# Feed-forward joins, the statistics of steps 41 and 42, and the back transposes of steps 34 to 42 in other slots

## The chip, the cores and the metric

One core of a Trainium2 chip runs the whole program. The metric is the device time of one launch in microseconds. The kernel before has a median of 708.54 us over three runs (708.42 to 709.91).

## The reference

The reference is a decoder block over four batches of 512 tokens with 512 features, in float32. There are 16 heads of 32 features, and every attention is causal.

```
x = x + self_attention(layernorm(x))          # q, k, v, o projections with biases
x = x + cross_attention(layernorm(x), ctx, ctx)   # no projections, keys and values are ctx
x = x + ffn(layernorm(x))
ffn(x) = relu(x @ W_up.T) @ W_down.T + sum(softmax(top2(x @ W_gate.T))) * (x @ W_expert)
```

## The kernel before

All engines follow one hand-made timetable of steps and slots. A step is one pair of heads (64 of them: 32 groups of four heads, two steps each), and has 8 slots, one for each head of the pair and block of 128 queries. The number of a slot is z = 8 * step + slot; below, "slot 41.5" is slot 5 of step 41. A slot is a place in each engine's program, not a time. Each engine runs its own program in order, and waits on semaphores for the others.

In slot i of step s:
- TensorE computes the score tile i of pair s + 1 (L500) into one of three banks, then runs what `RUNNING` gives it (a quarter of a projection or feed-forward job, "fill"; one quarter is three matmuls of 512 columns, or four transposes), and then turns a tile of probabilities of pair s (L514, four to one transposes) into a bank `t` or a free bank `m`.
- VectorE masks and reduces the score tile (L716), copies the turned tiles of slots 2, 3, 6 and 7 (L726), and empties the banks of jobs (`empty`).
- ScalarE takes the exponential (L944), copies the turned tiles of slots 0, 1, 4 and 5 (L953), and copies the high parts of the operands.
- GpSimd scales the probabilities of self-attention, makes the keys of cross-attention (`keys`, L1090 and L1092), and adds the result to the residual (`added`, L1100).
- SyncE issues the DMAs. `load_stack(s + 2)` lays out the operands of the scores two steps ahead.

At slot 0 of each even step TensorE first runs the **values burst** (`values`, L547: 16 small matmuls, 32 records), which closes the group of the two steps before. For a cross group ScalarE then copies it to `cn` in slot 2 (`context_hi`, L970), TensorE transposes it back into the same bank (`back`, L657, end of slot 4), VectorE scales it (`back_scaled`, L846, slot 5), and GpSimd adds it in the next step. In odd steps TensorE turns the queries of a coming group (`queries`, slot 1, L568), ScalarE and VectorE copy their high and low parts (`query_hi` in slot 3, L1007; `query_lo` in slot 5, L838). The values burst of the next even step waits for that `query_lo`, since both use the bank `pv`.

Cross-attention of batch f is done after step 8 (f + 5). Then its feed-forward part is fed in, one batch per eight steps: `f_stats_slots` (L750, L752) and `f_norm_slots` (L779) on VectorE, with `f_scale` on GpSimd (L1074, L1076) between them, then four turns of the normalised rows (`FL`, L568, at `turns_at`), whose high part ScalarE copies (L979) and whose low part VectorE subtracts (L802), then the gate (`FG`, L619), the up projection (`FU`), the expert (`FE`) and the down projection (`FD`), each in four jobs of four slots. The feed-forward matmuls are L553 to L555. VectorE adds the results of FE and FD to the residual (L828, L834). The jobs share two banks `m0` and `m1`: `plan()` gives each job the bank that is free first, and makes it wait until the job before it in that bank has been emptied. Score turns get a bank `m` where none of the jobs is near, else `t0` and `t1` in turn. `plan()` gives every job the same bank before and after the change; 147 of the 512 turns get another one, all from slot 42.5 on.

The normalisation ahead of cross-attention (`stats_slots`, `norm_slots`, L743 and L771) of batch j - 4 runs in the same way, with `ln_scale` (L1070) on GpSimd. The last group of batch 0 is 19 (steps 38 and 39, its back transposes in step 40). `f_stats_of(0, 0)` waits until GpSimd has added it.

## Time and profile before

| | us |
|---|---|
| median of three runs | 708.54 |
| lowest, highest | 708.42, 709.91 |
| profiled execution, time | 706.88 |
| profiled execution, span of the core | 705.0 |
| TensorE busy | 672.6 |
| ScalarE busy | 501.6 |
| VectorE busy | 494.4 |
| GpSimd busy | 257.1 |

All times in the rows below are counted from the start of the span of the profiled execution. The names PE, DVE, ACT and POOL are TensorE, VectorE, ScalarE and GpSimd. A row of a stretch (rows 2 and 4) has its borders and length, then busy time and instructions of PE, PEld (the weight loads), DVE, ACT and POOL, then PEclk, the busy share of the DMA engines and GB/s. A row of a timeline has start, length, engine, line, instruction and how many are merged. A value in square brackets is the idle time of the engine just before the instruction, with what ended it. PEclk is the granted TensorE clock as a share of 2.4 GHz.

### The profile page before, as it was taken

To read this page: it belongs to the slowest core of one execution; us is meant where nothing else is said; L and a number is where in the kernel's file an instruction comes from. 1 tells how busy PE (TensorE), PEld (TensorE's weight loads), DVE (VectorE), ACT (ScalarE), POOL (GpSimd) and SP (SyncE) were. 2 spreads that over 40 slices of the span, in tenths; PEclk is the share of its full clock that TensorE was granted. 3 is DMA by queue.
4 is the path that set the end of the run, shared out by engine and by line. 5 is a ranking of instruction groups with operands and counts; after the bars stand their busy time and mean duration, and the time that the engine had idled before them with its cause. 6 is when DMAs were issued, how large, how long until landed. Compare 5 with 4: busy or idle time off the path is not lost.

```text
span 705.0 us, 13884 instructions
## 1 busy us (share of the span) xinstructions
PE 672.6 (95%) x4488; PEld 520.1 (74%) x4488; DVE 494.4 (70%) x1730; ACT 501.6 (71%) x1450; POOL 257.1 (36%) x391
## 2 busy tenths in 40 slices
PE   6998999999999999999978988999999999999998
PEld 5776777777877777677756765777767887777786
DVE  6668766766766676767878779978867777764632
ACT  5778877777876778787898878877768876763110
POOL 4745645333555345751654432553202102000100
PEclk9999999999999999999999999999999999999999
DMA  9753533336433464354955776464435344320101
GB/s 315 193 151 75 141 70 91 77 93 184 117 71 91 127 196 98 88 123 124 268 140 144 195 215 144 120 166 104 113 98 156 100 105 106 69 96 1 59 1 60
DMA packets 52326, 86.12 MB, mean 122 GB/s; under 512 B 8608, under 2 KB 16800, under 8 KB 52256
## 3 DMA queue, kind: packets, MB, share of 16 engines
q1 hardware_dynamic: 52256, 85.25, 46.0%
q8 instruction: 36, 0.59, 0.3%
q14 instruction: 34, 0.28, 0.1%
HBM read 27.55 MB, written 7.34 MB: 49 GB/s over the span
## 4 chain that ended last, share of the span: by engine, by line
PE 80%; ACT 7%; DVE 6%; issue 2%; DMA 2%; POOL 2%; SPq 1%; ACTq 0%; POOLq 0%; DVEq 0%
PE t L514 15%; PE m L553 14%; PE m L554 14%; PE m L555 14%; PE pv L547 10%; PE s L500 8%; ACT probs L944 3%; DVE probs L716 2%; PE m L514 2%; ACT prob L953 2%; PE m L619 1%; DMA stack<-stage 1%; POOL probs L1057 1%; PE m L568 1%; DVE prob L726 1%
## 5 line engine op out<-in xcount | busy, mean ns | idle before, releaser
L716 DVE CUSTOM_DVE_ANT_0 probs<-s,mask 128x128 f32<-128x128 f32 (+3 forms) x512 | 246.5, 483 | 124.2 <-PE s L500 122.0
L944 ACT ACTIVATE probs<-probs,negmax 128x128 f32<-128x128 f32 (+3 forms) x512 | 284.7, 559 | 44.3 <-DVE negmax L716 43.6
L514 PE MATMUL t<-ident,probs 128*128 128x128 f32 x1116 | 198.0, 276 | 10.6 <-ACT prob L953 7.1
L500 PE MATMUL s<-stack 96*128 96x128 f32 (+3 forms) x512 | 196.5, 392 | 2.9 <-DMA stack<-stage 1.7
L1057 POOL TENSOR_SCALAR probs<-probs,rsum 128x128 f32<-128x128 f32 (+3 forms) x256 | 133.4, 539 | 176.4 <-DVE rsum L730 176.0
L953 ACT ACTIVATE prob<-t 128x384 f32<-128x384 f32 (+1 forms) x225 | 121.5, 541 | 87.1 <-PE t L514 85.5
L514 PEld LDWEIGHTS t<-ident,probs 128*128 128x128 f32 x1116 | 140.5, 141 | 57.4 <-ACT prob L953 11.0
L500 PEld LDWEIGHTS s<-stack 96*128 96x128 f32 x512 | 97.4, 190 | 14.1 <-DMA stack<-stage 2.4
L944 ACT ACTIVATION_READ_ACCUMULATOR probs<-probs,negmax 128x1 f32 x512 | 99.1, 194 | 0.0
L726 DVE COPY prob<-t 128x256 f32<-128x256 f32 (+1 forms) x215 | 76.3, 355 | 29.8 <-PE t L514 29.1
L553 PE MATMUL m<-xT_hi,w_lo 128*128 128x512 f32 x192 | 78.4, 409 | 1.2 <-DVE xT_lo L784 1.2
L554 PE MATMUL m<-xT_lo,w_hi 128*128 128x512 f32 x192 | 75.8, 395 | 0.0
L555 PE MATMUL m<-xT_hi,w_hi 128*128 128x512 f32 x192 | 75.6, 394 | 0.0
L553 PE MATMUL m<-w_hi,xT_lo 128*128 128x512 f32 x128 | 52.8, 413 | 0.0
L554 PE MATMUL m<-w_lo,xT_hi 128*128 128x512 f32 x128 | 50.5, 394 | 0.0
L555 PE MATMUL m<-w_hi,xT_hi 128*128 128x512 f32 x128 | 50.2, 393 | 0.0
L555 PEld LDWEIGHTS m<-xT_hi,w_hi 128*128 128x128 f32 x192 | 36.1, 188 | 8.6
L716 DVE DVE_READ_ACCUMULATOR2_ANT negmax<- 128x1 f32 x512 | 42.4, 83 | 0.0
L547 PE MATMUL pv<-prob,cv 128*32 128x128 f32 (+3 forms) x512 | 39.4, 450 | 1.6 <-ACT prob L953 1.4
L553 PEld LDWEIGHTS m<-xT_hi,w_lo 128*128 128x128 f32 x192 | 36.8, 191 | 2.7 <-DVE xT_lo L784 1.4
L554 PEld LDWEIGHTS m<-xT_lo,w_hi 128*128 128x128 f32 x192 | 36.5, 190 | 2.9
L547 PE MATMUL pv<-prob,V 128*32 128x128 f32 (+3 forms) x512 | 37.8, 435 | 0.0
(144 smaller groups left out, 956.6 us busy)
## 6 DMA issues: line engine op xcount, KB each, us to landing
stack<-stage SPq DMA_DIRECT2D x384, 128.0 KB, 2.3
xt<-in_x SPq DMA_DIRECT2D x16, 256.0 KB, 4.2
xres<-in_x SPq DMA_DIRECT2D x4, 1024.0 KB, 6.0
kraw<-in_ctxT SPq DMA_DIRECT2D x16, 256.0 KB, 3.0
cv<-in_ctx SPq DMA_DIRECT2D x16, 256.0 KB, 3.3
x<-xres SPq DMA_DIRECT2D x3, 1024.0 KB, 5.8
res<-x SPq DMA_DIRECT2D x8, 256.0 KB, 6.3
out<-res SPq DMA_DIRECT2D x2, 1024.0 KB, 4.7
```

The costliest lines, as they stand in the source:

```text
L500: nc.tensor.matmul(score_tile(P, i), stack[0:RS, P % 2, h, 0, chunk(qb)], stack[0:RS, P % 2, h, 1, 0:N], start=True, stop=True).then_inc(s ...
L514: mm = nc.tensor.transpose(dst[:, chunk(qb - kb)], probs[:, (2 * P + h) % 3, OFF[qb] + PART * kb:OFF[qb] + PART * kb + PART], ident[:, :])
L547: mm = nc.tensor.matmul(pv_bank[HD * j:HD * j + HD, PART * kb:T], v[:, HD * j:HD * j + HD], prob[kb][:, j, :], start=(kb == 0), stop=(kb = ...
L553: nc.tensor.matmul(dst, lhs[1], rhs[0], start=(c == 0), stop=False)
L554: nc.tensor.matmul(dst, lhs[0], rhs[1], start=False, stop=False)
L555: return nc.tensor.matmul(dst, lhs[0], rhs[0], start=False, stop=(c == KC - 1))
L568: mm = nc.tensor.transpose(dst[:, chunk(t)], src[:, t, chunk(c)], ident[:, :])
L716: nc.vector.tensor_tensor_reduce(probs[:, (2 * P + h) % 3, OFF[qb]:OFF[qb + 1]], score_tile(P, i), mask[:, T - N:T], -SCALE, BIG, ALU.add, ...
L726: nc.vector.tensor_copy(prob[kb][:, 2 * (P % 2) + h, :], turned_tile(P, i)).then_inc(t_dve, 1)
L944: nc.scalar.activation(tile, tile, ACT.Exp, bias=negmax[:, P % 2, h, qb:qb + 1], scale=-1.0, accum_out=total).then_inc(p_exp, 1)
L953: nc.scalar.activation(prob[kb][:, 2 * (P % 2) + h, :], turned_tile(P, i), ACT.Copy).then_inc(t_act, 1)
L1057: nc.gpsimd.tensor_scalar(tile, tile, rsum[:, P % 2, h, qb:qb + 1], 0.0, ALU.mult, ALU.add).then_inc(p_done, 1)
```

## The change

Five things move, all in the timetable; the arithmetic is the same.

- `back_slot`: the back transposes of the groups that end in steps 34 to 42 run in slot 5 instead of slot 4, and their scaling on VectorE in slot 6 instead of 5 (groups 16, 18, 19 and 20).
- The statistics of batch 0's feed-forward move from slots 41.1, 41.2, 41.4, 41.5 to 41.4, 41.6, 42.0, 42.0, its normalisation from 42.0, 42.0, 42.1, 42.1 to 42.4, 42.5, 42.6, 42.6. `f_scale(0)` on GpSimd moves from the end of step 41 into step 42, ahead of the wait for the normalisation and of `keys(23)`.
- The turns FL of batches 0, 1 and 2 start one slot later (from 43.1, 51.1, 59.1), the gate two slots later (44.4, 52.4, 60.4).
- The up projection follows: for batches 0 and 1 its four jobs start at 45.0, 45.5, 46.1, 46.6 instead of 44.6, 45.3, 46.0, 46.5, and the expert where it did (47.2); the last down job starts one slot later (51.6 instead of 51.5). For batch 2 all jobs from the gate on are two slots later.
- The statistics of batch 1's second norm move from 43.1 to 43.2 (the first one), its normalisation from 44.1, 44.4, 44.4, 44.5 to 44.3, 44.4, 44.5, 44.6.

```diff
--- before.py
+++ after.py
@@ -92,6 +92,11 @@
     return 2 * RANK[P // 2] + P % 2
 
 
+def back_slot(s):
+
+    return 3 if s >= NP else 5 if NPS + 2 <= s < PAIRS * (B + 1) + 3 else 4
+
+
 def feed_start(f):
 
     return FEED[f]
@@ -99,13 +104,13 @@
 
 def turns_at(f):
 
-    u = feed_start(f)
+    u = feed_start(f) + 1
     return [u + 3 * m for m in range(KC)]
 
 
 def gate_at(f):
 
-    return feed_start(f) + (8 if f == B - 1 else 10)
+    return feed_start(f) + (8 if f == B - 1 else 12)
 
 
 def route_at(f):
@@ -115,7 +120,7 @@
 
 def up_at(f, m):
 
-    return gate_at(f) + 4 + (4 if f >= B - 2 else 5) * m
+    return gate_at(f) + 4 + 4 * m + (0 if f >= B - 2 else (m + 1) // 2)
 
 
 def expert_at(f, m):
@@ -127,7 +132,7 @@
 
     if f >= B - 2:
         return expert_at(f, KC) + 4 * m
-    return expert_at(f, KC) + 5 * m if m < 2 else feed_start(f + 1) + 5 * (m - 2)
+    return expert_at(f, KC) + 5 * m if m < 2 else feed_start(f + 1) + 6 * (m - 2)
 
 
 def stats_slots(j):
@@ -137,7 +142,7 @@
         z -= 2 * PAIRS if j == B else 0
         return [z - 8, z - 7, z, z + 1]
     if j == B + 2:
-        return [z + 25, z + 28, z + 29, z + 31]
+        return [z + 26, z + 28, z + 29, z + 31]
     return [z, z, z + 16, z + 16] if j == B + 1 else [z, z, z + 1, z + 1]
 
 
@@ -149,20 +154,20 @@
     if j == B:
         return [z + 2, z + 3, z + 5, z + 6]
     if j == B + 2:
-        return [z + 33, z + 36, z + 36, z + 37]
+        return [z + 35, z + 36, z + 37, z + 38]
     return [z + 32, z + 32, z + 33, z + 33]
 
 
 def f_stats_slots(f):
 
     z = PAIRS * (PAIRS * (f + B + 1) + 1)
-    return [z + 1, z + 2, z + 4, z + 5]
+    return [z + 4, z + 6, z + 8, z + 8] if f == 0 else [z + 1, z + 2, z + 4, z + 5]
 
 
 def f_norm_slots(f):
 
     z = PAIRS * (PAIRS * (f + B + 1) + 2)
-    return [z, z, z + 1, z + 1]
+    return [z + 4, z + 5, z + 6, z + 6] if f == 0 else [z, z, z + 1, z + 1]
 
 
 END = (feed_start(B - 1) + UNITS) // PAIRS + 1
@@ -702,7 +707,7 @@
                             turn_gate(f)
                     if s % 2 == 1 and other((s + 3) // 2) and i == 1:
                         queries((s + 3) // 2)
-                    if s % 2 == 0 and other(s // 2 - 1) and i == (4 if s < NP else 3):
+                    if s % 2 == 0 and other(s // 2 - 1) and i == back_slot(s):
                         back(s // 2 - 1)
 
 
@@ -913,7 +918,7 @@
                         query_lo((s + 3) // 2)
                     if s % 2 == 0 and other(s // 2 - 1) and i == 1:
                         c_recip(s // 2 - 1)
-                    if s % 2 == 0 and other(s // 2 - 1) and i == (5 if s < NP else 4):
+                    if s % 2 == 0 and other(s // 2 - 1) and i == back_slot(s) + 1:
                         back_scaled(s // 2 - 1)
                     for j in range(1, 2 * B):
                         for t in range(NT):
@@ -1141,6 +1146,8 @@
                 if own(s // 2):
                     for qb in range(NT):
                         scaled(s, 1, qb)
+                if s == f_stats_slots(0)[-1] // PAIRS:
+                    f_scale(0)
                 for j in range(B + 1, 2 * B):
                     if s == norm_slots(j)[-1] // PAIRS:
                         pool.wait_ge(ln_done, NT * (j + 1))
@@ -1157,7 +1164,7 @@
                 for j in range(1, 2 * B):
                     if s == stats_slots(j)[-1] // PAIRS:
                         ln_scale(j)
-                for f in range(B):
+                for f in range(1, B):
                     if s == f_stats_slots(f)[-1] // PAIRS:
                         f_scale(f)
                 if 3 <= s < 3 + NT:
```

## Rows read from the trace of the kernel before

**Rows 1.** The page's section 1: busy time and share of the span.

```profile
PE 672.6 (95%) x4488; PEld 520.1 (74%) x4488; DVE 494.4 (70%) x1730; ACT 501.6 (71%) x1450; POOL 257.1 (36%) x391
```

**Rows 2.** Busy time by stretch, steps 41 to 44, one step a row.

```profile
417.30:424.41 7.11, 5.34 (x35) 3.85 (x33) 7.01 (x28) 7.11 (x24) 1.28 (x1) 1.00 1.05 288
424.41:433.88 9.47, 8.29 (x65) 5.16 (x65) 8.06 (x29) 6.27 (x21) 3.17 (x4) 0.82 0.66 158
433.88:442.47 8.59, 6.72 (x47) 5.02 (x46) 8.39 (x29) 8.59 (x28) 1.28 (x1) 1.00 0.34 86
442.47:453.57 11.10, 10.66 (x87) 8.00 (x88) 10.84 (x36) 9.31 (x29) 5.65 (x8) 1.00 0.54 131
```

**Rows 3.** TensorE's timeline, steps 40 to 44: start, length, instruction, idle before.

```profile
415.68 0.33 PE L657 MATMUL pv<-ident,cn 128*128 128x128 f32 x1 [0.90 <-ACT cn L970]
...
422.77 0.44 PE L500 MATMUL s<-stack 96*128 96x384 f32 x1 [0.86 <-DVE negmax L716]
...
424.41 0.30 PE L500 MATMUL s<-stack 96*128 96x128 f32 x1 [0.62 <-DMA stack<-stage]
...
432.20 0.33 PE L657 MATMUL pv<-ident,cn 128*128 128x128 f32 x1 [0.92 <-ACT cn L970]
...
448.29 0.50 PE L619 MATMUL m<-xT_hi,g_both 128*128 128x512 f32 x1 [0.43 <-ACT xT_hi L979]
```

**Rows 4.** Two stretches with granted clock; the values bursts of steps 42 and 44.

```profile
421.50:424.90 3.40, 1.73 (x9) 1.02 (x9) 3.33 (x13) 3.40 (x12) 0.00 (x0) 1.00 1.01 216
424.90:428.30 3.40, 3.33 (x20) 1.13 (x24) 3.37 (x12) 1.50 (x6) 1.29 (x2) 0.50 0.63 146
...
424.96 4.01 PE L547 MATMUL pv<-prob,cv 128*32 128x512 f32 x32 [0.26 <-DVE stage L838]
...
442.70 2.36 PE L547 MATMUL pv<-prob,cv 128*32 128x512 f32 x32
```

**Rows 5.** VectorE's timeline from the first statistics of batch 0 to step 42.

```profile
419.62 0.69 DVE L750 BATCH_NORM_STATS2 f_stats<-xt 128x6 f32<-128x512 f32 x1
...
420.44 0.53 DVE L716 CUSTOM_DVE_ANT_0 probs<-s,mask 128x384 f32<-128x384 f32 x1
...
424.18 0.68 DVE L838 TENSOR_TENSOR stage<-pv,stage 128x512 fp32r<-128x512 f32 x1
...
426.99 0.29 DVE L726 COPY prob<-t 128x128 f32<-128x128 f32 x1
...
427.40 1.00 DVE L779 TENSOR_SCALAR f_xln<-xt,f_mv,f_rstd 128x512 f32<-128x512 f32 x2
429.73 0.42 DVE L716 CUSTOM_DVE_ANT_0 probs<-s,mask 128x256 f32<-128x256 f32 x1 [1.33 <-PE s L500]
```

**Rows 6.** ScalarE's timeline: the query copy of step 41.

```profile
422.67 0.60 ACT L1007 ACTIVATE stage<-pv 128x512 fp32r<-128x512 f32 x1
```

**Rows 7.** VectorE's timeline, norms in step 44; GpSimd splits weights from 446.71 to 450.66.

```profile
446.78 0.82 DVE L771 TENSOR_SCALAR V<-res,mv,rstd 128x512 f32<-128x512 f32 x1 [0.19 <-POOL rstd L1070]
...
449.94 1.46 DVE L771 TENSOR_SCALAR V<-res,mv,rstd 128x512 f32<-128x512 f32 x2
```

**Rows 8.** TensorE's timeline in steps 51, 52 and 59.

```profile
512.76 0.44 PE L568 MATMUL m<-ident,f_xln 128*128 128x128 f32 x2 [0.76 <-DVE xt L834]
...
516.60 0.40 PE L553 MATMUL m<-w_hi,w_lo 128*128 128x512 f32 x1
...
517.07 0.40 PE L555 MATMUL m<-w_hi 128*128 128x512 f32 x1
517.65 0.66 PE L568 MATMUL m<-ident,f_xln 128*128 128x128 f32 x4 [0.18 <-DVE xT_lo L802]
...
519.60 0.51 PE L553 MATMUL m<-w_hi,w_lo 128*128 128x512 f32 x1 [0.55 <-DVE xt L834]
...
528.43 0.74 PE L619 MATMUL m<-xT_hi,g_both 128*128 128x512 f32 x2 [0.19 <-DVE xt L834]
...
594.30 0.55 PE L568 MATMUL m<-ident,f_xln 128*128 128x128 f32 x3 [0.76 <-DVE res L834]
```

## The prediction, made before the change was run

> **What bounds the kernel now.** I read the page's first section, then the engines in stretches one step long, then each engine's own timeline where TensorE stood still. The page shows TensorE busy for 95% of the span, with VectorE and ScalarE at 70% and 71% [rows 1]. So over the whole span an edit pays only where it takes idle time off TensorE, or lets the engine that starves it finish earlier. I took the first score matmul of each step as the step's start (the start times are the borders in [rows 2]). By that the steps that the change touches are of two kinds.
>
> Steps 41 to 44 are not bound by TensorE. In step 41 it works 5.34 us of 7.11, in 42 8.29 of 9.47, in 43 6.72 of 8.59. VectorE works 7.01 of 7.11, 8.06 of 9.47, 8.39 of 8.59 and, in step 44, 10.84 of 11.10 [rows 2]. VectorE stands still for only 0.10 + 1.41 + 0.20 + 0.26 = 1.97 us in four steps. ScalarE has no idle time at all in steps 41 and 43. The TensorE stalls here (0.90, 0.86, 0.62, 0.92, 0.43 us [rows 3]) are therefore mostly a symptom: they can only be gained so far as VectorE and ScalarE also get ahead. Steps 51, 52, 59 and 60 are different: there TensorE has no other idle time than a few stalls behind the chain of feed-forward banks [rows 8], and the others have room. In steps 45 to 50 and 53 to 58 the timeline shows no stall of TensorE at all, so nothing can be gained there.
>
> **The clock.** From 424.9 to 428.3 us the granted clock is 0.50, the lower level of 1.2 GHz, after a stretch in which TensorE worked 1.73 of 3.40 us [rows 4]. The values burst that opens step 42 fell into it and took 4.01 us; the same 32 matmuls took 2.36 us at the full clock, so 1.65 us went to it.
>
> **Part 1: back transposes one slot later (steps 34, 38, 40, 42).** A back transpose waits for ScalarE's copy cn. The wait is 0.90 us in step 40 and 0.92 us in step 42 [rows 3]; the back transposes of 34 and 38 show no idle time at that line, so I cost them at nothing (34 and 35 wait for GpSimd, 38 is full). One slot later, the score tile and turn of slot 5 stand ahead of it and cover the 0.9 us. But ScalarE runs without a gap after each values burst, and TensorE catches up with it in the next step. I count 0 for the removed waits themselves, with 1.8 us as the other end. The scaling goes behind one more score tile and copy on VectorE (about 0.8 us later); who waits for it is the query transpose of slot 1 in the next step and GpSimd's addition, and neither stands behind it in the trace of before, so I cost that at nothing; if the room is gone, it is those 0.8 us.
>
> **Part 2: statistics of batch 0 from slots 41.1, 41.2, 41.4, 41.5 to 41.4, 41.6, 42.0, 42.0.** One costs VectorE 0.82 us (419.62 to 420.44 [rows 5]). Ahead of query_lo in slot 41.5 stood three, now one, so VectorE could start it 1.64 us sooner than 424.18, at 422.54. But query_lo waits for ScalarE's query copy, 422.67 + 0.60 = 423.27 [rows 6], and ScalarE is gapless. So query_lo moves by 0.91 us, not 1.64. Behind it the count of statistics ahead of the copy of slot 41.7 (426.99) is unchanged, so that ends at 427.28 - 0.91 = 426.37. Then one score tile (0.2) and the two statistics of 42.0 (1.64) fill the time in which TensorE runs the values burst: VectorE is ready at 428.2, where before it stood idle for 1.33 us and resumed at 429.73 [rows 5]. TensorE's burst ends near 427.0 if the clock stays up, near 427.8 if it falls again; either way VectorE is last. **Gain at the start of slot 42.1: 1.5 us.**
>
> **Part 3: normalisation of batch 0 from 42.0, 42.0, 42.1, 42.1 to 42.4 to 42.6.** Two of the four stood in the burst's shadow (1.00 us for two at 427.40 [rows 5]). Now all four stand behind it, on an engine that has 0.2 us to spare until step 44: a loss of 1.0 us. What remains when the values burst of step 44 ends is 1.5 - 1.0 = **0.5 us**. f_scale is two small operations on a GpSimd that works 3.17 of 9.47 us in step 42 [rows 2], and four score tiles of VectorE (0.3 to 0.6 us each) stand between the statistics and slot 42.4, so I count no wait. GpSimd's wait for f_xln now holds back keys(23) by half a step; the stack load that needs them is issued in step 44, so that is at nothing too.
>
> **Part 4: joins of batch 0 one to two slots later.** The gate's wait for xT_hi (0.43 us, at 448.29 [rows 3]) has one more slot of distance and goes. Two job slots of the up projection leave step 44 for steps 45 and 47. A job slot is three matmuls at 0.235 us (516.60 to 517.07 for two [rows 8]), 0.7 us. TensorE's step 44 gets 1.4 us lighter than VectorE's 10.84 us, so VectorE bounds it, and the 0.7 us that land past step 45 are paid there: up to 0.7 us back. Against it VectorE's own waits in step 44 (0.26 us) go, and its norms shift away from GpSimd's weight split: beside it they took 0.82 and 1.46 us for three, where one alone takes 0.5 [rows 5, 7], so about 0.7 us of VectorE time may come back. The Trainium skill has this as a lock (SBUF — State Buffer, on the port pair that DVE and GpSimd share: a VectorE operation in a two-port mode and one of GpSimd block each other for its whole length). The trace fits it: norms over-long only where GpSimd works. Part 4 sums to 0.43 + 0.26 + 0.7 - 0.7 = 0.7 us at best and -0.3 at worst; I take **0.4 us**. Steps 41 to 47 together: 0.5 + 0.4 = **0.9 us**.
>
> **Part 5: joins of batches 1 and 2 (steps 51, 52 and 59, 60).** The first turn of the next batch waits 0.76 us for a bank that VectorE empties at slot 51.0; in slot 51.1 a turn, a score tile and a down slot (some 1.6 us) stand ahead: gone. The last down job waits 0.55 us for its bank, one slot more: gone. The gate waits 0.19 us, one slot more: gone. That is 1.50 us. Against it: the second turn waited 0.18 us for xT_lo although the last down slot (0.7 us) stood between them in slot 51.3 [rows 8]. In slot 51.4 it stands alone behind a score tile. That cover is lost, and the copy ahead is 0.15 us shorter: the stall grows to 0.18 + 0.7 - 0.15 = 0.7, so 0.5 to 0.6 us is given back. Net 0.95 us per pair of steps, bounds 0.8 and 1.5. Steps 59 and 60 run the same program for the next batch and show the same stall of 0.76 us at its place [rows 8]: **1.9 us** for both. Batch 2's two job slots that move behind step 63 are work of the same length in another place.
>
> **The sum.** 0.9 + 1.9 = 2.8 us. The profiled execution has a span of 705.0 and a time of 706.88 us, 1.66 us under the median of the three runs, 708.54; some run-to-run difference of this size (one fallen clock stretch is worth as much) is there. I apply the 2.8 us to the median: 708.54 - 2.8 = **705.7 us**, and a new span near 702.2 beside a profile like this one.
>
> **The rivals.** *All that TensorE waits for is gained.* Then 0.90 + 0.86 + 0.62 + 0.92 + 0.43 = 3.7 us, the clock's 1.65 and twice 1.50, or 8.4 us: 700.1. For it: the stalls stand on the very engine that is busy for 95%. Against: VectorE's 1.97 us of idle time in steps 41 to 44 is all that can be taken there unless its work shrinks. Chance 0.10; half-way to it lies 702.8.
> *The new stalls eat the gain.* The second turn's wait takes over what the first gives (0.3 us left each time), and in 41 to 47 the norms' 1.0 us and the up slots' 0.7 us cancel the 1.5: 708.0, within 0.2%. That the slots were already covered, so that nothing moves, ends here too. Chance 0.25.
> *Slower: VectorE in steps 42 to 45.* If ScalarE's query copy comes no sooner and VectorE's two statistics outlast the burst, nothing is gained at 42.1, and the 1.0 us of norms and the 0.7 us of up slots are paid in full; with batches 1 and 2 at nothing the time is 708.54 + 1.7 = 710.2. It decides once VectorE resumes after the burst of step 42 later than 1.0 us after TensorE offers it the score tile. The clock adds to it: TensorE would stand still for 3 us in step 43 instead of 1.87, and a stretch at 0.5 there costs up to 1.65 us. Chance 0.15.
>
> **How the numbers follow.** The forecast (704 to 707.1) has 0.50, the full gain 0.10, no difference 0.25, slower 0.15. The lower end takes in half of the full gain (702.8), the upper one the no-difference case and part of the slower one (709.2). What a measurement can tell from no change is 0.2%, 1.4 us: faster 0.60, same 0.25, slower 0.15.
>
> **What would show it.** In the trace after: no wait of the back transposes for cn in steps 40 and 42; query_lo of step 41 right behind ScalarE's copy; two statistics in the shadow of the values burst and no VectorE idle time there; VectorE busy for all of step 43, and the burst of step 44 ending about 0.5 us sooner. In steps 51 and 59 the first turn and the last down job without a wait, and the second turn with one of 0.6 to 0.8 us. If TensorE's idle time in step 43 grows while the step ends later, the slower case holds; if the second turn waits no longer than before, the gain is nearer to 4 us.

## The result: 0.25% slower

The changed kernel has a median of 709.69 us over 21 runs (707.59 to 711.93), the kernel before beside it 708.38 us, also over 21 (705.51 to 711.59). The ratio is 1.0025, with a 95% interval of 1.0013 to 1.0036 (the two medians by themselves give 1.0018). The prediction was 705.7 us, with a range of 702.8 to 709.2. The profiled execution has a time of 708.46 us and a span of 706.6. Two executions of the kernel before beside the experiments took 838 and 1097 us at a mean granted clock of 0.75 and 0.56, and no figure here counts them.

The page's section 1 for the changed kernel answers to [rows 1]:

```profile
PE 672.4 (95%) x4488; PEld 520.3 (74%) x4488; DVE 492.1 (70%) x1730; ACT 501.6 (71%) x1450; POOL 257.2 (36%) x391
```

All engines run the same instructions, and none is busy for longer by more than 0.2 us; what grew is time in which TensorE waits. The busy times by step, 41 to 47, with columns as in [rows 2]:

```profile
417.43:425.26 7.83, 5.25 (x35) 3.79 (x33) 6.97 (x27) 7.83 (x25) 1.28 (x1) 1.00 1.05 310
425.26:432.25 6.99, 6.67 (x64) 4.69 (x65) 6.89 (x28) 5.37 (x19) 1.29 (x2) 1.00 1.03 225
432.25:441.36 9.11, 6.70 (x47) 5.13 (x45) 8.34 (x30) 9.11 (x29) 3.14 (x3) 1.00 0.35 89
441.36:451.86 10.50, 9.29 (x77) 6.41 (x78) 10.20 (x32) 7.91 (x26) 5.18 (x6) 1.00 0.60 138
451.86:462.03 10.17, 9.45 (x58) 7.72 (x58) 8.61 (x34) 8.69 (x27) 7.61 (x9) 1.00 0.34 82
462.03:473.26 11.23, 11.23 (x87) 8.32 (x86) 6.20 (x27) 7.56 (x22) 2.96 (x3) 1.00 0.77 209
473.26:482.45 9.19, 9.01 (x55) 7.37 (x54) 7.16 (x27) 7.43 (x23) 8.43 (x9) 1.00 0.28 71
```

Steps 45 and 47 of the kernel before, for comparison:

```profile
453.57:461.69 8.12, 8.12 (x54) 6.92 (x52) 7.71 (x30) 6.97 (x22) 7.88 (x8) 1.00 0.54 148
472.92:481.05 8.13, 8.13 (x53) 6.94 (x51) 5.75 (x23) 6.65 (x21) 7.27 (x8) 1.00 0.32 81
```

Step 42 is 2.5 us shorter and step 44 0.6 us, but step 45 is 2.05 us longer, 47 1.06, 41 0.72 and 43 0.52. The table sets the lengths beside those of all experiments. A length is from the first score matmul of a step to that of the next, read off each trace. The last three columns are sums; step 40 takes 7.43 us with the back transposes in their old slot and 6.98 in the new one. Kernels marked * had TensorE's granted clock at 0.50 for 3.4 or 6.8 us in steps 41 to 43. So columns 41 to 43 are to be compared among those without a mark.

```
us                      step 41    42    43    44    45    46    47 | 40-43  44-47  51-56
before *                   7.11  9.47  8.59 11.10  8.11 11.23  8.13 | 32.60  38.57  62.91
loads_later                7.11  8.24  8.59 11.10  8.11 11.23  8.13 | 31.37  38.57  62.90
after                      7.83  6.99  9.11 10.50 10.17 11.23  9.19 | 30.91  41.09  63.36
joins_only                 7.34  7.94  8.66  9.61 10.18 11.25  9.19 | 31.37  40.23  63.38
joins_before               7.14  7.79  9.84 11.19  8.11 11.23  8.14 | 31.75  38.67  62.91
back_only                  8.40  7.51  8.60 11.16  8.12 11.23  8.15 | 31.49  38.66  62.91
stats_only *               8.08  9.20  9.92 11.18  8.11 11.23  8.14 | 34.63  38.66  62.88
loads_and_back             7.39  8.24  8.59 11.10  8.11 11.23  8.15 | 31.20  38.59  62.91
loads_later_back_stats *   5.90  9.41  9.83 11.96  8.11 11.23  8.15 | 32.12  39.45  62.89
after_loads_later *        5.90  8.69 10.21 10.56 10.19 11.25  9.20 | 31.78  41.20  63.36
no_m_turns                 7.58  7.77  8.60 11.10  8.11 11.23  8.14 | 31.37  38.58  62.93
gate_one *                 8.99  8.63  9.12 11.98 10.46 11.19  8.12 | 33.72  41.75  63.37
one_gate_moved             5.90  8.68  9.29 11.81  9.92 11.22  8.14 | 30.85  41.09  62.93
up_before *               10.51  9.74  9.11 11.79  9.92 11.22  8.14 | 36.34  41.07  64.40
norm6_before *             8.05  8.69  9.12 10.00 10.16 11.25  9.20 | 32.84  40.61  63.34
norm6_only                 7.11  8.24  8.60 11.73  8.11 11.23  8.14 | 31.37  39.21  62.88
norm7_earlier *            8.47  9.73  9.12 10.47 10.18 11.25  9.19 | 34.30  41.09  62.98
f_norm_earlier *           8.74  9.64  8.93 10.48 10.19 11.25  9.20 | 34.29  41.12  63.35
```

The row loads_later is the kernel before in all but two loads of data, and without the fallen clock; so it is the fair base at full clock. Against it the change takes 0.46 us off steps 40 to 43, adds 2.52 in 44 to 47 and 0.46 in 51 to 56, and takes 0.32 off from step 59 to the end. That is 2.2 us of the 2.5 between the two spans (706.6 and 704.1); most of the rest (0.23 us) is in the start-up, where no instruction is changed.

The waits of TensorE in the changed kernel, from its timeline in steps 40 to 60 (they answer to [rows 3, 8]):

```profile
416.26 0.66 PE L662 MATMUL pv<-ident,cn 128*128 128x128 f32 x4 [0.32 <-ACT cn L975]
...
425.26 0.33 PE L505 MATMUL s<-stack 96*128 96x128 f32 x1 [2.02 <-DMA stack<-stage]
...
431.09 0.66 PE L662 MATMUL pv<-ident,cn 128*128 128x128 f32 x4 [0.32 <-ACT cn L975]
...
434.78 0.63 PE L573 MATMUL m<-ident,f_xln 128*128 128x128 f32 x4 [0.97 <-DVE f_xln L784]
...
444.81 0.43 PE L552 MATMUL pv<-prob,cv 128*32 128x128 f32 x8 [0.77 <-DVE prob L731]
...
453.64 0.66 PE L519 MATMUL t<-ident,probs 128*128 128x128 f32 x4 [0.72 <-DVE prob L731]
...
474.49 0.66 PE L519 MATMUL t<-ident,probs 128*128 128x128 f32 x4 [0.18 <-DVE prob L731]
...
518.99 0.66 PE L573 MATMUL m<-ident,f_xln 128*128 128x128 f32 x4 [0.92 <-DVE xT_lo L807]
...
530.83 0.74 PE L624 MATMUL m<-xT_hi,g_both 128*128 128x512 f32 x2 [1.12 <-DVE xt L839]
```

The waits that were to go are gone: the gate's 0.43 us in step 44, the first turn's 0.76 and the last down job's 0.55 us in step 51. The back transposes wait 0.32 us for 0.90. New are 2.02 us for a DMA, 0.97 us for the normalised rows, 0.77 us inside the burst of step 44, 0.72 us in slot 45.0, 0.18 us in 47.0 and 1.12 us at the gate of step 52. The second turn of step 51 waits 0.92 us instead of 0.18.

### The profile page after: what moved, and what is told of

The parts are those of the page before. It is cut to its first block, busy times and chain, and to the rows that moved or that the text cites. A ratio compares the mean times of both kernels' runs of the same rounds, so it can differ in the third digit from the quotient of the medians.

```text
span 706.6 us, 13884 instructions
## 1 busy us (share of the span) xinstructions
PE 672.4 (95%) x4488; PEld 520.3 (74%) x4488; DVE 492.1 (70%) x1730; ACT 501.6 (71%) x1450; POOL 257.2 (36%) x391
## 4 chain that ended last, share of the span: by engine, by line
PE 77%; DVE 10%; ACT 6%; issue 3%; DMA 2%; POOL 2%; SPq 1%; DVEq 0%; POOLq 0%; ACTq 0%
PE t L519 15%; PE m L558 14%; PE m L559 13%; PE m L560 13%; PE pv L552 9%; PE s L505 8%; DVE probs L721 3%; ACT probs L949 3%; ACT prob L958 1%; DVE prob L731 1%; PE m L519 1%; DMA stack<-stage 1%; POOL probs L1062 1%; PE m L573 1%; DVE xT_lo L807 1%
## 5 line engine op out<-in xcount | busy, mean ns | idle before, releaser
L519 PE MATMUL t<-ident,probs 128*128 128x128 f32 x1134 | 201.6, 276 | 11.7 <-ACT prob L958 6.1
L519 PEld LDWEIGHTS t<-ident,probs 128*128 128x128 f32 x1134 | 142.6, 141 | 60.6 <-ACT prob L958 10.6
L958 ACT ACTIVATE prob<-t 128x384 f32<-128x384 f32 (+1 forms) x229 | 123.6, 540 | 83.0 <-PE t L519 82.3
```

The lines of the kernel that those rows point to most:

```text
L519: mm = nc.tensor.transpose(dst[:, chunk(qb - kb)], probs[:, (2 * P + h) % 3, OFF[qb] + PART * kb:OFF[qb] + PART * kb + PART], ident[:, :])
L958: nc.scalar.activation(prob[kb][:, 2 * (P % 2) + h, :], turned_tile(P, i), ACT.Copy).then_inc(t_act, 1)
```

## Experiments

### Which part: joins_before, joins_only, back_only, stats_only

These take the change apart. The first is the changed kernel with the joins (and the second norm of batch 1) in their old slots, the second the reverse. The other two move the back transposes alone, or the statistics, normalisation and `f_scale` of batch 0 alone.

```diff
 # joins_before, against after
-    u = feed_start(f) + 1
+    u = feed_start(f)
 ...
-    return feed_start(f) + (8 if f == B - 1 else 12)
+    return feed_start(f) + (8 if f == B - 1 else 10)
 ...
 # and up_at, down_at, stats_slots, norm_slots as before
 # back_only, against before: back_slot as in the change
 # stats_only, against before: f_stats_slots, f_norm_slots, f_scale(0) as in the change
```

> The changed kernel with the feed-forward joins and the statistics and norms of steps 43 and 44 back where they were; the back transposes and the statistics and norms of steps 41 and 42 stay moved. Theory A (the joins lose the time: in the traces steps 44 to 47 are 2.5 us longer and steps 51 to 56 0.4 us longer): the 1.6 us gained by the first score tile of step 43 stay, and the time is 1 to 2 us under the kernel before. Theory B (VectorE is overloaded by the four norms of batch 0 behind the burst of step 42, and the loss shows in steps 44 and 45): steps 44 and 45 stay long, and the time is no better than the kernel before.

> The kernel before with only the joins and the statistics and norms of steps 43 and 44 moved. Theory A: steps 44 to 47 are 2 to 2.5 us longer than before and steps 51 to 56 0.4 us, steps 59 to the end 0.3 us shorter: 2 to 3 us slower than before. Theory B: 0 to 2 us faster, because 1.5 us of bank stalls go in steps 51, 52 and again in 59, 60.

> The kernel before with only the four back transposes and their scaling one slot later. If ScalarE and VectorE set the pace after each values burst, the waits of 0.90 and 0.92 us for cn shrink, but the first score tile of steps 42 and 44 starts no more than 0.3 us sooner than before. If TensorE's waits are the path, these start 0.6 and 1.2 us sooner.

> The kernel before with only the statistics and the normalisation of batch 0 moved. If VectorE is the bound of steps 41 to 43, nearly the whole gain by the start of step 43 is here (1.3 us or more sooner at its first score tile), half of it lost again in step 43, where the four norms stand. If the back transposes carried it, less than 0.5 us is here.

Measured: joins_before 709.83 us, ratio 1.0022 (1.0002 to 1.0042), span 704.2. joins_only 708.41 us, ratio 1.0022 (1.0003 to 1.0040), span 706.1. back_only 706.72 and stats_only 709.36 us, one run each.

What follows: the loss from step 44 on belongs to the joins. joins_only has it in full in steps 45, 47 and 51 to 56; joins_before, back_only and stats_only have none of it (at most 0.10 us in steps 44 to 47). The other half of the change gives nothing back. At full clock joins_before even spends 0.38 us more than the base in steps 40 to 43. It waits 1.32 us for a stack load and 2.13 us for the normalised rows:

```profile
423.87 0.33 PE L505 MATMUL s<-stack 96*128 96x128 f32 x1 [1.32 <-DMA stack<-stage]
...
434.09 0.63 PE L573 MATMUL m<-ident,f_xln 128*128 128x128 f32 x4 [2.13 <-DVE f_xln L784]
```

The turn of the joins one slot later is what brings the second wait down to 0.97 us in the changed kernel: so the two halves do fit together, only that each costs.

The medians alone would have told less: joins_before and joins_only both have the ratio 1.0022. But joins_before has a span of 704.2 us in the execution at full clock, and only 2 of its 12 executions ran without a fallen clock, while 8 had a mean of 0.995 or lower (12 of 23 of the kernel before beside it). Its loss over the base at full clock is 0.48 us in steps 40 to 47; the rest of what its median shows lies in executions with a fallen clock. It had been expected to be 1 to 2 us faster than the kernel before, and joins_only 2 to 3 us slower, where the steps give 1.8 (1.66 + 0.48 - 0.34).

### Is it the DMA: loads_later, loads_later_back_stats, loads_and_back, after_loads_later

In the issue timeline of SyncE (SPq) for the changed kernel, the expert's weights and the residual rows go out at 413.08 and 414.86 us, ahead of the stack load of pair 43 at 417.27:

```profile
408.63 3.77 SPq L418 DMA_DIRECT2D stack<-stage  x6
412.45 0.58 SPq L424 DMA_DIRECT2D kraw<-in_ctxT  x1
413.08 1.69 SPq L433 DMA_DIRECT2D V<-in_expert  x1
414.86 2.29 SPq L407 DMA_DIRECT2D res<-x  x4
417.27 3.96 SPq L418 DMA_DIRECT2D stack<-stage  x6
```

That stack load's first half lands at 425.2 us by its semaphore, and the first score tile of step 42 starts at 425.26. In the other traces with these loads ahead of it the landing and the start are likewise 0.1 us apart (before 424.3 and 424.41, joins_only 425.1 and 425.16, joins_before 423.8 and 423.87), with one exception, norm6_only, below. The edit issues the bulk loads one step later.

```diff
-                if s == SELF_END + 3:
+                if s == SELF_END + 4:
                     sp.wait_ge(f_lo_done, KC)
                     load_weight("expert", EXPERT)
                     ...
                     load_x(res2, x2[2])
```

loads_later is the kernel before with it, loads_and_back adds the back transposes, loads_later_back_stats adds the statistics too, after_loads_later is the changed kernel with it.

> The kernel before with one edit: the loads of the expert weights and of the residual of batch 2 (2 MB) are issued in step 41, behind the stack load of pair 43, instead of in step 40 ahead of it. In all six traces so far the first score tile of step 42 starts within 0.1 us of the landing of that stack load (423.8 to 425.5 us). Theory D (the bulk loads hold back the stack load, and that sets the start of step 42): it lands near 419, the first score tile of step 42 starts 0.5 to 1.5 us sooner than 424.4, bound then by VectorE's queue, and the median falls by 0.5 to 1.5 us. Rival: VectorE is just as late there (its score tile 42.5 ends at 424.33 in the trace before), and nothing changes.

> The same edit on top of joins_before (back transposes and statistics moved, joins as before). Theory D: with the stack load out of the way the moved statistics show their worth: the first score tile of step 42 starts at 423 or sooner, and step 43, where the turns wait for the late norms, keeps its 9.8 us; the time is under loads_later by up to 0.5 us at full clock. Rival: the late norms cost what the start of step 42 gains, and the two are the same.

> The kernel before with the back transposes one slot later and the bulk loads of step 40 issued in step 41 behind the stack load. At full clock loads_later needs 31.4 us from the first score tile of step 40 to that of step 44, back_only 31.5 us with its stack load 1.3 us late. Theory G (VectorE is the bound of steps 40 to 43, the transfer comes second): step 40 is 6.98 us as in back_only, step 41 takes back half or more of that, and steps 40 to 43 are 30.9 to 31.2 us. If TensorE's waits for cn are the path, they are 30.3 us or less.

> The changed kernel with the bulk loads behind the stack load. Theory D, part two: in the changed kernel VectorE is ready before the stack load lands, so here the order of the loads decides. Step 41 falls from 7.83 us to about 5.9 us; VectorE and ScalarE (the copy of the queries) bound the burst behind it, which takes about 1 us back in step 42. Net 0.5 to 1.2 us sooner by the first score tile of step 43. Rival: nothing comes of it, since the burst waits for ScalarE's query copy anyway.

Measured: loads_later 707.69 us, ratio 0.9998 (0.9978 to 1.0018). loads_later_back_stats 707.82 us, 1.0003 (0.9987 to 1.0019). loads_and_back 707.74 us, 0.9993 (0.9980 to 1.0005). after_loads_later 708.94 us, one run. The first line is TensorE in loads_later, the second in loads_later_back_stats:

```profile
424.67 0.30 PE L500 MATMUL s<-stack 96*128 96x128 f32 x1 [0.62 <-DVE negmax L716]
```

```profile
424.19 2.14 PE L552 MATMUL pv<-prob,cv 128*32 128x512 f32 x24 [1.05 <-DVE stage L843]
```

What follows: in the kernel before, the DMA and VectorE ended the wait of 0.62 us at the same time. With the load landed early (418.1 us) the wait is unchanged, and only its releaser has another name. norm6_only (last section) shows the same with the bulk loads ahead: its stack load landed at 427.32 us, and TensorE started 0.42 us after that, again after a wait of 0.62 us:

```profile
427.74 0.30 PE L505 MATMUL s<-stack 96*128 96x128 f32 x1 [0.62 <-DVE negmax L721]
```

With the statistics moved as well, step 41 takes 5.90 us, 1.93 less than in the changed kernel: it was the DMA that kept the changed kernel from this. But the burst then waits 1.05 us for `query_lo`, which waits for ScalarE. In after_loads_later the clock is at 1.00 until step 43, step 41 is 1.93 us shorter than in the changed kernel and step 42 is 1.70 us longer, so that step 43 begins only 0.23 us sooner, where 0.5 to 1.2 had been expected. In loads_later_back_stats step 44 grows by 0.86 us over before as well. At the end of step 47 loads_later_back_stats is 1.6 us behind loads_later and after_loads_later 3.0 us, each with the clock at 0.50 for 3.4 us in step 43. The DMA hides a gain that the next engine takes back; it isn't the cause of the loss. None of these kernels is measurably faster than the one before.

### Is it the lost m banks: no_m_turns

From slot 42.5 on many turns get another bank after the change. The edit takes the free `m` banks away from all turns from step 44 on, with nothing else changed.

```diff
-                if z > PAIRS and all(end + 2 <= z or start >= z + 4 ...
+                if z > PAIRS and z < PAIRS * 44 and all(end + 2 <= z or ...
```

> The kernel before, but no turn of a score tile from step 44 on may use a bank of the jobs: the 19 or so that do in steps 44 to 58 alternate on the two t banks. It tests why steps 47 and 55 grew by 1.06 us for one added job slot of 0.70 us. Theory E (the job slots moved close together leave no free bank, and the turn of slot 47.0 waits for VectorE's copy of slot 46.6): steps 46, 47, 54, 55 grow by 0.2 to 0.4 us each pair with all joins in place. Rival (the added job slot itself costs it): no step changes by more than 0.05 us.

Measured: 707.83 us, and no step from 43 on differs by more than 0.02 us from before. The lack of these banks costs nothing by itself; with the joins moved as well it wasn't tried.

### Is it the job slots or the gate: gate_one, one_gate_moved, up_before

gate_one puts the gate one slot sooner than the change does. up_before keeps turns and gate of the change for batches 0 and 1, puts their up projection back where it was (from 44.6), and batch 2's joins too. one_gate_moved moves only batch 0's turns and gate, and issues the bulk loads later.

```diff
 # gate_one, against after
-    return feed_start(f) + (8 if f == B - 1 else 12)
+    return feed_start(f) + (8 if f == B - 1 else 11)
 ...
-    return gate_at(f) + 4 + 4 * m + (0 if f >= B - 2 else (m + 1) // 2)
+    return gate_at(f) + 4 + (4 * m if f >= B - 2 else (0, 5, 10, 14, 19)[m])
 # up_before, against after: up_at; and turns_at and gate_at of batch 2, down_at of batch 1 as before
-    return gate_at(f) + 4 + 4 * m + (0 if f >= B - 2 else (m + 1) // 2)
+    return feed_start(f) + (12 if f == B - 1 else 14) + (4 if f >= B - 2 else 5) * m
```

> The changed kernel with the gate one slot later than before instead of two, and the up projection one slot later for its first job, its last at the old place (46.5, 54.5). Theory A: one job slot instead of two is pushed out of steps 44 and 52, and the gate's four back transposes (0.44 us) stay in steps 44 and 52, so steps 45 and 53 are near 8.8 us instead of 10.2 and 9.2; the loss of steps 44 to 47 against before halves. The gate's wait behind the down job in step 52 grows from 1.12 to about 1.8 us, since it has one slot less.

> A version built from what the runs gave: back transposes and statistics moved, bulk loads behind the stack load, the turns and the gate of batch 0 moved as in the changed kernel, but its up projection and all joins of batches 1 and 2 where they were before. Theory A: no job slot leaves steps 44, 52 and 60, so steps 44 to 47 take 38.6 us as before (40.1 in joins_only), steps 51 to the end are as before, and the turns of step 43 wait for the norms under 1 us instead of 1.7. Then the time at full clock is 0.8 to 1.5 us under the kernel before. If the gate itself, and not the up projection, is what costs time, step 44 grows by more than 1 us.

> The changed kernel with the up projection of batches 0 and 1 where it was before (44.6 and on), gate and turns moved, and batch 2's joins as before. Theory A: with the job slots back, steps 44 to 47 together lose less than 0.5 us against before instead of 1.7, and steps 51 to 56 gain 0.7 us, what the bank stalls gave less the new wait of the turn in slot 51.4. Rival: the gate's later place makes the loss, steps 44 to 47 stay 1.5 us longer or more.

Measured: gate_one 712.29 us and up_before 716.56 us (one run each); one_gate_moved 708.87 us, ratio 1.0014 (1.0000 to 1.0027). With the up projection back, step 47 is back at 8.14 us and step 45 falls only to 9.92, while step 44 is 11.8 us. Steps 44 to 47 sum to 41.07 to 41.09 us in both kernels, as much as in the changed one. By that the place of the two job slots wouldn't decide. But both kernels have a wait that neither the kernel before nor the changed one has. This is TensorE in one_gate_moved, in slot 45.3:

```profile
457.71 0.50 PE L558 MATMUL m<-xT_hi,w_lo 128*128 128x512 f32 x1 [1.13 <-DVE w_lo L826]
```

The late gate still holds one of the two `m` banks at slot 45.3, so `plan()` gives the second up job the bank of the first, and it waits until VectorE has emptied the first (L826). In the kernel before and in the changed kernel the two jobs have different banks. Slot 45.3 takes 2.44 us in both these kernels and 1.05 in the changed one. Without these 1.39 us the sum would be near 39.7 us (an estimate), 1.1 over the 38.57 of before. So the test doesn't separate the gate from the job slots. That the sums are equal is a coincidence of two different losses, and how the 2.5 us divide between them was not shown by an experiment. In up_before the same wait stands once more for batch 1, 1.14 us in step 53, and steps 51 to 56 take 64.40 us.

gate_one was expected to halve the loss of steps 44 to 47. They take 41.75 us, more than in the changed kernel (41.09). The gate waits 1.16 us for the copy of the turned rows (L984) in slot 44.4, and in slot 45.5 a turn into a bank `m` waits 0.98 us for L826.

up_before's own high time is something else. Its stack load landed at 429.1 us and TensorE stood still for 4.70 us:

```profile
429.13 0.48 PE L505 MATMUL s<-stack 96*128 96x128 f32 x1 [4.70 <-DMA stack<-stage]
```

### Is it VectorE's norms: norm6_before, norm6_only, norm7_earlier, f_norm_earlier

```diff
 # norm6_before, against after (norm6_only: the reverse, against before)
-        return [z + 26, z + 28, z + 29, z + 31]
+        return [z + 25, z + 28, z + 29, z + 31]
 ...
-        return [z + 35, z + 36, z + 37, z + 38]
+        return [z + 33, z + 36, z + 36, z + 37]
 # norm7_earlier, against after (norm_slots)
+    if j == B + 3:
+        return [z + 36, z + 37, z + 38, z + 38]
 # f_norm_earlier, against after (f_norm_slots)
-    return [z + 4, z + 5, z + 6, z + 6] if f == 0 else [z, z, z + 1, z + 1]
+    return [z + 3, z + 4, z + 5, z + 5] if f == 0 else [z, z, z + 1, z + 1]
```

In spite of its label, norm7_earlier moves the norms of step 52 behind the emptying of the last down job.

> The changed kernel with the statistics and the normalisation of batch 1's second norm in their old slots (first statistic in 43.1, norms in 44.1, 44.4, 44.4, 44.5); the joins stay changed. Theory A (the norms' later slots make VectorE late, so the turn of slot 45.0 waits 0.7 us for its copy): that wait falls under 0.2 us, and steps 44 to 47 take 40.3 us or less where the changed kernel takes 41.09. Theory B (the gate's later place with its turns makes it): the wait stays near 0.7 us and steps 44 to 47 stay within 0.3 us of 41.1.

> The kernel before with only those statistics and norms moved as in the change (43.2 and 44.3, 44.4, 44.5, 44.6). Theory A: steps 44 to 47 grow by 0.5 to 1.0 us over the 38.57 of before. Theory B: they stay within 0.1 to 0.2 us of 38.57, and the joins alone carry the 1.66 us that the kernel with all joins loses there.

> The changed kernel with the norms of batch 2's second norm... those of step 52 that stand ahead of the emptying of the last down job, moved behind it, to slots 52.4, 52.5, 52.6 and 52.6. Theory: the gate's wait of 1.12 us in step 52 is VectorE's emptying behind two norms; it falls to the 0.71 us of step 60, where no norm stands there, and step 52 gets 0.3 to 0.5 us shorter. Rival: the wait is that of the down job's own end and stays at 1.1 us.

> The changed kernel with the normalisation of batch 0 one slot earlier (42.3, 42.4, 42.5, 42.5 for 42.4, 42.5, 42.6, 42.6). If the first turn of step 43 waits 0.97 us only because the norms are late, the wait falls to about 0.3 us; TensorE's 0.77 us of waits in step 44 behind VectorE stay or shrink by up to 0.5. If VectorE is simply full, the wait shows up at the score tiles of step 42 instead, and steps 42 to 44 together stay within 0.2 us of the changed kernel's 26.60.

Measured, one run each: 712.19, 709.62, 711.01 and 711.45 us. All but the second have a stretch at 0.50 in step 42 (norm6_only has its own far from here, from 10.8 and from 358.9 us on), so the steps decide. One fence for each of norm6_before, norm7_earlier and f_norm_earlier, TensorE's timeline:

```profile
457.30 0.66 PE L519 MATMUL t<-ident,probs 128*128 128x128 f32 x4 [0.71 <-DVE prob L731]
```

```profile
533.34 0.73 PE L626 MATMUL m<-xT_hi,g_both 128*128 128x512 f32 x2 [0.71 <-DVE xt L841]
```

```profile
438.44 0.55 PE L519 MATMUL t<-ident,probs 128*128 128x128 f32 x3 [0.92 <-DVE prob L731]
```

What follows:
- The late norms of batch 1 cost 0.5 to 0.6 us in step 44, from both sides: 10.50 to 10.00 when put back, 11.10 to 11.73 when moved alone. The wait of slot 45.0 is untouched (0.71 us), as theory B has it; the sum of steps 44 to 47, 40.61, lies between A's 40.3 and B's 41.1. Neither theory held as written. The 2.5 us of these steps are made of three: joins_only loses 1.66, of which these norms are 0.5 and the turns, gate and jobs some 1.1; the other 0.86 (41.09 to 40.23) comes with batch 0's late statistics and norms. By themselves, in joins_before, these cost 0.10 us there and more in step 43: with the turns a slot later the wait for them is handed on into step 44.
- The gate's wait in step 52 falls from 1.12 to 0.71 us and the step from 11.52 to 11.11. The two norms ahead of the emptying cost 0.41 us; the 0.71 that remain are the emptying itself.
- With the rows of batch 0 normalised a slot earlier, the feed-forward turn no longer waits, but the score turn behind it does, 0.92 us for VectorE's copy. Steps 42 to 44 sum to 29.05 us, against 29.32 in norm7_earlier, which has the same low stretch of the clock and the norms late. VectorE was full; the wait is handed on.

## Why the prediction was wrong, step by step

The term of part 2 was mis-sized, and parts 4 and 5 left out what the moved jobs cost where they land. The rest held.

**What bounds the steps: right.** Steps 41 to 43 are bound by VectorE and ScalarE (ScalarE works 7.83 of 7.83 us in step 41, VectorE 6.89 of 6.99 in step 42, ScalarE 9.11 of 9.11 in step 43), and the sum of the stalls there was no gain. The sentence that nothing can be gained in steps 45 to 50 and 53 to 58 was right too; what I left out is that much can be lost there.

**Part 1, back transposes: 0, right.** Of 0.90 us, 0.58 are gone and step 40 is 0.45 us shorter, but step 41 takes 0.28 back (loads_and_back: 7.39 for 7.11 us). What stays is 0.17 us (31.20 for 31.37 in steps 40 to 43), less than a measurement can tell.

**Part 2, statistics: +1.5 us, in fact +0.36; mis-sized.** Here is VectorE's timeline in the changed kernel, which answers to [rows 5]:

```profile
421.94 0.69 DVE L755 BATCH_NORM_STATS2 f_stats<-xt 128x6 f32<-128x512 f32 x1
...
423.88 0.69 DVE L843 TENSOR_TENSOR stage<-pv,stage 128x512 fp32r<-128x512 f32 x1 [0.71 <-ACT stage L1012]
...
427.10 0.69 DVE L755 BATCH_NORM_STATS2 f_stats<-xt 128x6 f32<-128x512 f32 x1
...
427.92 0.66 DVE L755 BATCH_NORM_STATS2 f_stats<-xt 128x6 f32<-128x512 f32 x1
...
428.72 0.39 DVE L721 CUSTOM_DVE_ANT_0 probs<-s,mask 128x256 f32<-128x256 f32 x1
```

`query_lo` waits for ScalarE's copy, 13.43 us after the start of step 40 instead of 14.31: 0.88 sooner, where I had 0.91. Two statistics fill the burst, and VectorE resumes without a gap 18.27 us after the start of step 40, instead of 19.86 (429.73 [rows 5], step 40 starting at 409.87). That is 1.59 us sooner, where I had 1.5. But in loads_later, which has the slots of before and the full clock, VectorE resumes at 428.76, with step 40 starting at 410.13: 18.63. So 1.23 of the 1.59 us was the fallen clock of the one execution that I read, which I named in a paragraph of its own and then left in the term. At full clock the statistics are worth 0.36 us. The idle time of 1.33 us that they were to fill isn't there at full clock. This is loads_later, where the first score tile of slot 42.1 follows the norms without a gap:

```profile
427.66 1.00 DVE L779 TENSOR_SCALAR f_xln<-xt,f_mv,f_rstd 128x512 f32<-128x512 f32 x2
428.76 0.42 DVE L716 CUSTOM_DVE_ANT_0 probs<-s,mask 128x256 f32<-128x256 f32 x1
```

So behind `query_lo` the two statistics of slot 42.0 (0.82 us each) only took the place of two norms (1.00 us together). The stack load has no part in this: VectorE resumes 18.28 us after the start of step 40 in joins_before, where it lands late, and in after_loads_later, where it lands early.

I also missed what else ended the same wait. The row of 0.62 us [rows 3] names the DMA of the stack as releaser. I took it for one of VectorE's stalls because VectorE was busy; both ended together. With VectorE sooner, the DMA was last, and TensorE waited for it for 2.02 us. On this the Trainium skill has the page DMA: Bandwidth & Descriptors (Queues, rings and completion order): on each of the DMA engines the descriptors of one ring are consumed in ring order. The traces agree: all these loads are issued by SyncE, and the last DMA of that half of the stack lands 2.4 us after its issue where it goes ahead of the bulk loads (loads_later, at 418.1 us), and 6.3 to 9.4 us after it behind them (at 423.8 us or later).

**Part 3, norms of batch 0: -1.0 us, right in size.** Over steps 40 to 47, statistics, norms and back transposes together cost 0.48 us in joins_before (against loads_later) and 0.40 in the changed kernel (against joins_only). Less the 0.17 of the back transposes and the 0.36 of part 2 that is a price of 0.9 to 1.0 us for the norms. The three parts were to give 0.5 us and took 0.4, and nearly all of the difference is part 2. Who would wait for the norms I didn't say. The four norms stand on a full engine. The first turn of step 43 waits 0.97 us for them, and the burst of step 44 0.77 us for the copies behind them and behind `xT_lo`. Step 44 is 0.89 us longer than in joins_only (10.50 to 9.61). In joins_before the first turn waits 2.13 us.

**Part 4, joins of batch 0: +0.4 us, in fact -1.7 (joins_only, steps 44 to 47).** Here the mechanism failed, and by as much as in part 5. The price of a job slot was right, and so was that two of them move past step 45. The lengths of the slots, again from first score matmul to first score matmul, show what was wrong:

```
us              0    1    2    3    4    5    6    7
step 44 before  2.94 0.89 0.85 1.50 1.46 0.91 1.08 1.48
   joins_only   3.34 0.45 0.84 0.83 1.45 0.91 0.86 0.94
step 45 before  1.24 1.58 0.40 1.05 1.25 1.14 1.10 0.34
   joins_only   2.19 2.03 1.09 1.04 0.53 1.15 1.10 1.05
step 47 before  1.25 0.89 1.10 1.05 1.25 1.15 0.40 1.05
   joins_only   1.64 1.59 1.08 1.05 1.24 1.14 0.40 1.05
```

A slot in step 45 or 47 is 0.70 us longer with a job slot in it than without (45.2, 45.7, 47.1), and 0.72 shorter where one left (45.4). Step 44 loses two job slots and the gate's back transposes (`turn_gate`), 1.4 + 0.45 us at these prices, and its wait of 0.43 us: 2.3 us in all. It gave back 1.49. Slots 44.6 and 44.7 are only 0.22 and 0.54 us shorter since two quarters of the gate, some 0.47 us each, now stand where the up quarters stood. The other 0.8 us went to VectorE, which is busy for 9.30 us of 9.60 in joins_only: slot 44.0 is 0.40 us longer, and 0.26 us of waiting come back in slot 44.3.

```profile
444.33 0.43 PE L552 MATMUL pv<-prob,cv 128*32 128x128 f32 x8 [0.18 <-DVE prob L731]
...
447.11 0.33 PE L519 MATMUL t<-ident,probs 128*128 128x128 f32 x1 [0.26 <-DVE negmax L721]
```

I charged "up to 0.7 us" for the job slots, and three things in steps 45 and 47 I didn't count. The gate's back transposes move with it, from slot 44.7 to 45.1: 0.45 us. TensorE now comes to slot 45.0 sooner than VectorE, and waits 0.72 us; the slot is 0.95 us longer, and nothing else in it changed. And in 47.0 the turn waits 0.18 us behind a weight copy and the scaling of `cn`, 0.69 and 0.68 us on VectorE in the same slot, and the slot is 0.39 us longer. The differences over 45 and 47 are 0.95 + 0.45 + 0.69 - 0.72 + 0.71 + 0.39 + 0.70 = 3.17 us (the other slots stay within 0.02); the two steps grew by 2.07 + 1.06 = 3.13. Less the 1.49 of step 44 that is 1.64 us. This account is read off the slots of joins_only; the experiments separate only the norms of batch 1 from the rest of it.

VectorE ahead of slot 45.0, in the changed kernel:

```profile
450.02 1.35 DVE L776 TENSOR_SCALAR V<-res,mv,rstd 128x512 f32<-128x512 f32 x1
...
451.64 0.68 DVE L851 TENSOR_TENSOR cn<-pv,c_rsum 128x512 f32<-128x512 f32 x1
...
452.24 0.53 DVE L776 TENSOR_SCALAR V<-res,mv,rstd 128x512 f32<-128x512 f32 x1
...
453.17 0.41 DVE L731 COPY prob<-t 128x256 f32<-128x256 f32 x1
453.51 0.53 DVE L776 TENSOR_SCALAR V<-res,mv,rstd 128x512 f32<-128x512 f32 x1
```

The copy of 453.17 is what the turn of 45.0 waits for. The norm of 450.02 still takes 1.35 us beside GpSimd's weight split, 0.82 more than the one at 452.24. The 0.7 us that were to come back when the norms shift away from the split didn't: the four norms took 0.82 + 1.46 + 0.53 = 2.81 us before, and 0.59 + 1.35 + 0.53 + 0.53 = 3.00 after. GpSimd's split waits for the same statistics and moved along with the norms. That VectorE and GpSimd lock each other out, as the Trainium skill has it in the place that the prediction names (SBUF — State Buffer), still fits the rows: 1.35 us beside the split, 0.53 away from it.

**Part 5, batches 1 and 2: +1.9 us, in fact -0.46 and +0.32.** Steps 51 and 59 went as predicted in their waits: 0.76 and 0.55 us gone, and the second turn waits 0.92 us (0.7 predicted). The gate's 0.19 us [rows 8] was called gone, "one slot more". It grew to 1.12 us. The last down job had moved by a slot as well, and its emptying on VectorE with it, behind two norms:

```profile
528.46 0.91 DVE L776 TENSOR_SCALAR V<-xres,mv,rstd 128x512 f32<-128x512 f32 x2
529.28 0.55 DVE L721 CUSTOM_DVE_ANT_0 probs<-s,mask 128x384 f32<-128x384 f32 x1
529.76 0.08 DVE L721 DVE_READ_ACCUMULATOR2_ANT negmax<- 128x1 f32 x1
529.76 0.42 DVE L731 COPY prob<-t 128x256 f32<-128x256 f32 x1
530.10 0.68 DVE L839 TENSOR_TENSOR xt<-m,xt 128x512 f32<-128x512 f32 x1
```

norm7_earlier puts the norms behind it, and 0.41 us of the wait is gone. The larger omission is in steps 53 and 55. Batch 1's up projection moves just as batch 0's does, two job slots and the gate's back transposes, and I had worked that out for batch 0 only. Steps 53 and 55 grew by 1.08 and 1.06 us, and all that steps 51 and 52 gave (1.39 and 0.34) went there. For batch 2 the same slots moved behind step 63, where they cost what they weigh (1.4 us), and no other wait stood against them; it is the only part that gained.

**The sum.** 2.8 us were forecast. At full clock the traces give -2.2: +0.46 for steps 40 to 43, -2.52, -0.46 and +0.32. By the parts of the prediction that is -0.4 for parts 1 to 3 (forecast +0.5), -1.7 for part 4 (+0.4) and -0.1 for part 5 (+1.9). The median lost only 1.3 us, which the next section bears on. The rival that held in its sign was "VectorE in steps 42 to 45", with its price of up slots paid in full. Its condition, that nothing is gained at 42.1, nearly held at full clock, where 0.36 us was gained instead of 1.5, but not for its reason: ScalarE's query copy did come sooner, by 0.88 us. The norms' 1.0 us was paid as it says, and the joins took 1.66 where it has 0.7. That batches 1 and 2 stay at nothing is near what was seen.

## What to carry to other kernels

Before moving work from one place to the next, ask of both places which engine ends last there: work that leaves a place bound by another engine gives back little, and costs its full length where its own engine is the bound. Move a chain in thought with all that hangs on it (the emptying, the back transposes, the next batch's copy of it), and for each named wait that will go, name the event that ends second. A term read off one execution with a fallen clock has to be worked out again at the full clock before it is laid on a median.

## What the runs showed of the hardware

**The clock fell where TensorE had no long gap, and stayed up over a longer one.** In the kernel before, the granted clock goes to 0.50 after a stretch in which TensorE worked 1.73 of 3.40 us [rows 4] and stood still for at most 0.86 us at a time. In the changed kernel it waited 2.02 us in one piece at nearly the same place, and the clock stayed at 1.00. So the longest single wait isn't what tells. What such a stretch cost in step 42 is 9.47 - 8.24 = 1.23 us (before against loads_later).

**The executions counted of the changed kernel had fewer of them.** Each execution lists its mean granted clock, and one stretch of 3.4 us at 0.50 in 705 us lowers it by 0.0024. Grouped by that number (mean span, number of executions; before is taken from the runs beside the experiments, and one at 0.990 with 709.6 us is left out of the table):

```
clock   1.000        0.998        0.997        0.995        0.993
before  704.2 (9)    705.7 (10)   705.1 (14)   706.4 (26)   708.0 (8)
after   706.8 (9)    708.0 (7)    -            709.6 (5)    -
```

At the full clock the change costs 2.7 us, near the 2.5 between the two spans. But 9 of 21 executions of it ran at 1.000, and 9 of 68 of the kernel before. That fits a median that shows only 1.3 us. The two counts weren't taken side by side, and the count of the kernel before itself varies (5, 3 and 1 of 23 beside the three sets of experiments). Side by side, joins_only has 2 of 12 and the kernel before 5 of 23; one_gate_moved has 5 of 12 and the kernel before 1 of 23. So that the change makes the clock fall less often is not shown, and why it would wasn't settled: in joins_before, which waits 3.62 us in step 43, 5 of 12 executions were at 0.993 or lower, which fits TensorE's idle time as the cause but doesn't show it.

**A landing time on a shared queue varies by microseconds.** In thirteen traces the stack load of pair 43 is issued behind the same two bulk loads. It landed 14.1 us (joins_before) to 17.5 us (up_before) after the start of step 40. In twelve of them step 42 began 0.04 to 0.12 us after it; in norm6_only, where it landed after 14.1 us and VectorE was later, 0.42 us after it.
